# Second stage of a gated cross-attention kernel: down weights turned by transposing transfers, token factors in three bf16 parts, clip after rounding, first products by halves

## The chip, the cores and the metric

The kernel runs on one core of one Trainium2 chip. The metric is the device time of one execution in microseconds (us). Three runs of the kernel before gave 1939.12, 1939.28 and 1939.48 us; the median is 1939.28 us. The trace is of a further, profiled execution.

## The reference, cut to what matters

Two gated layers act on x of 4 x 1024 tokens with 512 features: a cross-attention over 64 text tokens with tanh, a quantized gated feed-forward, a second cross-attention with 16 heads, and a ternary feed-forward with a depthwise convolution. The part around the change is the quantized gated feed-forward:

```python
def _act_fake_quant(x, clip_factor):
    scale = sigmoid(clip_factor) * max(abs(x)) / 127.0
    return clip(round(x / scale), -128, 127) * scale
def _weight_fake_quant(w):
    scale = max(abs(w), axis=1) / 127.0
    return clip(round(w / scale), -128, 127) * scale
xq   = _act_fake_quant(x, clip_x[0])                       # x: layer-normed, 4096 x 512
gate = einsum('bsh,ih->bsi', xq, _weight_fake_quant(w_gate))   # 1408 x 512
up   = einsum('bsh,ih->bsi', xq, _weight_fake_quant(w_up))
h    = _act_fake_quant(silu(gate) * up, clip_down[0])
out  = einsum('bsi,hi->bsh', h, _weight_fake_quant(w_down))    # 512 x 1408
```

The scale of xq is one number for all tokens, and so is that of h: each needs the maximum over everything before the first value can be quantized. The weights w1 and w2 of the ternary feed-forward are also prepared here: mean of |w| over the whole matrix, then round(w / mean) clipped to -1, 0, 1.

## The kernel before, in words

The program has three stages on the same five engines; the order on each engine is written out by hand, one function for each engine and stage (`vector_A`, `vector_B`, `vector_C` and so on), and semaphores tie them. Stage A (up to about 963 us) is the first cross-attention; stage B (about 963 to 1151 us) computes silu(gate) * up and prepares weights; stage C is the rest. All DMAs are issued by SyncE (SP), in program order, each behind its own waits.

Between A and B stands a short chain. The layer norm's factor of every token, `ln1_scale` (128 tokens x 32 tiles), is turned by TensorE (L712) and copied to `cT` (L482); the largest value goes through `diagA` (L480) and a product with ones (L714) to all partitions, and VectorE forms `q_scale` (L484 to L490) and from it the scales `gs` and `us` (L867, L868).

Stage B works on four blocks of 1024 tokens, each in two halves of 512. The block index is o, and within a block i runs over 11 groups of 128 inner channels; n = 11 o + i runs from 0 to 43. For a half, TensorE spreads the token factors over the partitions (`rows`, four fp32 products of 128 columns, L1036), VectorE multiplies (`scaled`, L876), clips (L883) and rounds to bf16 (L888) into `xqT`. These three steps of block o + 1 stand behind the steps i = 2, 3, 4 and 6, 7, 8 of block o; for block 0 they stand ahead of the loop. For each n, TensorE forms 8 products for gate (L1060) and 8 for up (L1066), each 128 x 512; gate of n waits for h of n - 2, up of n waits for silu of n - 1. ScalarE computes silu (L1021), VectorE silu * up into `h` (L916) and the row maxima (L920), and SP stores h (L1156) to DRAM.

Beside this, three chains run in slots of n:

- Down weights, in four groups r of 128 rows, one group each 11 steps: load, VectorE's row maximum (L897), scale and reciprocal, ScalarE's scaling with the rounding constant (L987), eleven 128 x 128 fp32 transposes on TensorE in three turns through PSUM bank 7 (L1047), each copied by ScalarE to bf16 `wdT` (L991).
- Ternary weights, first pass from n = 1: 16 parts of 512 KB are loaded (L1125) into a ring of four buffers, ScalarE takes |w| (L1000), GpSimd adds it up (L1094); behind n = 19 VectorE sums over the columns (L933, twice), behind n = 20 TensorE spreads the sums through bank 6 (L1076), and behind n = 21 VectorE forms the means (L937, L940).
- Ternary weights, second pass: the same 16 parts are loaded again; from n = 23 ScalarE scales and rounds one part in each step (L1007), GpSimd clips it (L1098), and two steps later ScalarE writes fp8 (L1014). The load of a part waits for the fp8 write that frees its buffer; in SP's order it stands one step after that write and one step ahead of its use.

At the end the maximum of `hmax` goes through `diagB` (L955) and a product with ones (L1083) to `q_scale`, and stage C's first loads of h wait for `b_done`.

## Time and profile before

| | |
|---|---|
| median of three runs | 1939.28 us |
| profiled execution, its own time | 1936.77 us |
| span of its trace | 1934.9 us |
| mean granted TensorE clock in the span | 0.982 of full |
| TensorE busy | 1589.2 us, 82% |
| VectorE busy | 1715.7 us, 89% |
| ScalarE busy | 1477.4 us, 76% |
| GpSimd busy | 612.7 us, 32% |

The profiled execution lies 2.51 us below the median of the runs, and its span 1.87 us below its own time. PE is TensorE, PEld its weight loads, DVE VectorE, ACT ScalarE, POOL GpSimd, SPq SyncE's queue. A row of the timeline gives the start, the duration, the engine, the line, the operation, the tiles written and read, how many alike were merged, and in brackets the idle time just before with what ended it. A merged row of k instructions gives the time from the first start to the last end.

### The profile page before, as it was taken

To read this page: it belongs to the slowest core of one execution; us is meant where nothing else is said; L and a number is where in the kernel's file an instruction comes from. 1 tells how busy PE (TensorE), PEld (TensorE's weight loads), DVE (VectorE), ACT (ScalarE), POOL (GpSimd) and SP (SyncE) were. 2 spreads that over 40 slices of the span, in tenths; PEclk is the share of its full clock that TensorE was granted. 3 is DMA by queue.
4 is the path that set the end of the run, shared out by engine and by line. 5 is a ranking of instruction groups with operands and counts; after the bars stand their busy time and mean duration, and the time that the engine had idled before them with its cause. 6 is when DMAs were issued, how large, how long until landed. Compare 5 with 4: busy or idle time off the path is not lost.

```text
span 1934.9 us, 24513 instructions
## 1 busy us (share of the span) xinstructions
PE 1589.2 (82%) x9474; PEld 721.2 (37%) x9542; DVE 1715.7 (89%) x2616; ACT 1477.4 (76%) x1099; POOL 612.7 (32%) x480
## 2 busy tenths in 40 slices
PE   7778965698557976696499977999999987899996
PEld 4222211132112211231144434666666653444442
DVE  6999999999999998889688877899999867999997
ACT  4999999999999999999544754555454436888881
POOL 1000000000000000000043225666666643899991
PEclk9999999999999999999889989999999999999999
DMA  5001100020000010000079754333333111122212
GB/s 204 1 22 32 57 12 1 23 77 18 6 1 1 17 60 1 1 6 6 16 270 341 278 192 148 99 109 115 114 99 111 44 55 39 44 77 77 66 55 76
DMA packets 116709, 143.65 MB, mean 74 GB/s; under 512 B 25326, under 2 KB 74606, under 8 KB 116210
## 3 DMA queue, kind: packets, MB, share of 16 engines
q1 hardware_dynamic: 116594, 142.10, 22.3%
q8 instruction: 75, 1.23, 0.3%
q14 instruction: 40, 0.33, 0.1%
HBM read 87.55 MB, written 50.33 MB: 71 GB/s over the span
## 4 chain that ended last, share of the span: by engine, by line
ACT 44%; PE 32%; DVE 14%; POOL 4%; issue 4%; DMA 3%; SPq 0%; another core or an unknown queue 0%; DVEq 0%; POOLq 0%; ACTq 0%
ACT unit L546 40%; PE psum L1729 5%; PE psum L1763 5%; PE psum L1715 3%; PE psum L1066 3%; PE psum L1060 3%; DVE unit L457 2%; POOL h L1904 2%; PE psum L1739 2%; PE psum L1756 2%; DVE psum L1495 2%; PE psum L1786 1%; DVE psum L1500 1%; POOL hidden L1921 1%; PE psum L1748 1%
## 5 line engine op out<-in xcount | busy, mean ns | idle before, releaser
L546 ACT ACTIVATE unit<-unit 128x4096 f32<-128x4096 f32 x244 | 857.5, 3613 | 0.5 <-DVE unit L457 0.3
L457 DVE TENSOR_SCALAR unit<-feat_proj,text_proj 128x1024 f32<-128x1024 f32 x976 | 667.9, 749 | 64.3 <-PE psum L686 61.5
L686 PE MATMUL psum<-unit,w_pad 128*32 128x512 f32 x3904 | 471.8, 601 | 226.5 <-ACT unit L546 226.3
L686 PEld LDWEIGHTS psum<-unit,w_pad 128*32 128x32 f32 x3904 | 102.2, 109 | 542.0 <-ACT unit L546 384.9
L729 POOL TENSOR_SCALAR red<-red 128x8 f32<-128x8 f32 x4 | 2.0, 507 | 531.5 <-DVE red L332 531.5
L1786 PE MATMUL psum<-xq_block,w_q 128*128 128x512 bf16 x489 | 121.3, 388 | 16.1 <-ACT h L1662 11.2
L1904 POOL TENSOR_TENSOR h<-h,arow 128x512 f32<-128x512 f32 x104 | 125.5, 1231 | 20.4 <-ACT h L1662 20.4
L729 POOL TENSOR_SCALAR rstd<-mv 128x8 f32<-128x8 f32 (+1 forms) x5 | 1.7, 334 | 403.2 <-DVE mv L227 403.2
L598 PE MATMUL psum<-xnT,W_sb 128*128 128x512 f32 x256 | 123.4, 610 | 1.9 <-ACT xnT L500 1.9
L1637 ACT ACTIVATE scores<-scores 128x1024 f32<-128x1024 f32 x32 | 33.9, 1058 | 114.0 <-POOL scores L1890 114.0
L1921 POOL TENSOR_TENSOR hidden<-hidden,srow 128x2048 f32<-128x2048 f32 x28 | 114.3, 4083 | 10.1 <-DVE hidden_q L1530 9.8
L1729 PE MATMUL psum<-xnT_c,wq_sb 128*128 128x256 f32 x512 | 115.7, 379 | 1.2 <-ACT xnT_c L1624 1.2
L1763 PE MATMUL psum<-wo_sb,attn_outT 128*128 128x512 f32 x256 | 115.4, 593 | 0.0
L1818 PE MATMUL psum<-w_q,hidden_q 128*128 128x512 fp8e4 x448 | 101.3, 379 | 13.5 <-DVE x3in L1543 9.1
L1729 PEld LDWEIGHTS psum<-xnT_c,wq_sb 128*128 128x128 f32 x512 | 96.0, 190 | 20.2 <-issue 6.7
L1679 ACT ACTIVATE hidden<-psum 128x512 f32<-128x512 f32 x112 | 69.5, 640 | 27.3 <-DVE psum L1500 27.3
L1715 PE MATMUL psum<-wdT,hq 128*128 128x512 bf16 x323 | 78.7, 393 | 14.1 <-DVE hq L1427 11.1
L1667 ACT ACTIVATE psum<-h,conv_b_sb,conv_w_sb 128x512 f32<-128x512 f32 x112 | 86.6, 791 | 2.4
L1495 DVE SCALAR_TENSOR_TENSOR psum<-h,conv_w_sb,psum 128x512 f32<-128x512 f32 x112 | 82.9, 750 | 5.8 <-ACT psum L1667 5.7
L1060 PE MATMUL psum<-xqT,wgT 128*128 128x512 bf16 x348 | 84.0, 384 | 4.7 <-DVE xqT L888 3.7
L1021 ACT ACTIVATE silu<-psum,gs 128x1024 f32<-128x1024 f32 x44 | 48.7, 1108 | 49.8 <-PE psum L1060 47.3
L1066 PE MATMUL psum<-xqT,wuT 128*128 128x512 bf16 x340 | 83.3, 383 | 0.9 <-ACT silu L1021 0.3
(260 smaller groups left out, 2761.0 us busy)
## 6 DMA issues: line engine op xcount, KB each, us to landing
h_scratch<-h SPq DMA_DIRECT2D x44, 512.0 KB, 4.2
hin<-h_scratch SPq DMA_DIRECT2D x32, 704.0 KB, 4.7
xin<-in_x SPq DMA_DIRECT2D x8, 1024.0 KB, 5.7
tern_in<-in_w1T SPq DMA_DIRECT2D x16, 512.0 KB, 5.1
tern_in<-in_w2T SPq DMA_DIRECT2D x16, 512.0 KB, 7.0
x<-in_x SPq DMA_DIRECT2D x16, 512.0 KB, 3.7
x_scratch<-x SPq DMA_DIRECT2D x32, 256.0 KB, 2.0
x3in<-x_scratch SPq DMA_DIRECT2D x31, 256.0 KB, 3.0
```

The costliest lines, as they stand in the source:

```text
L457: ins = ve.tensor_scalar(units[:, n % 3, k, :], FP[:, bi % 2, k, :], TP[:, k, n:n + 1], None, ALU.add)
L546: ac.activation(units[:, n % 3], units[:, n % 3], ACT.Tanh).then_inc(unit_tanh, 1)
L598: mm = te.matmul(psum[:, banks[j], :], W_sb[:, k, m * P:(m + 1) * P], xnT[:, k, half * BANK:(half + 1) * BANK], start=(k == 0), stop=(k == ...
L686: mm = te.matmul(psum[k * TG:(k + 1) * TG, 3 + 2 * grp + half, :], w_pad[:, k, TG - 1 - tt:2 * TG - 1 - tt], units[:, n % 3, k, half * BAN ...
L1060: mm = te.matmul(gate_pair(n)[:, half, :], wgT[:, k, i * P:(i + 1) * P], xqT[:, o % 2, k, half * BLK:(half + 1) * BLK], start=(k == 0), st ...
L1066: mm = te.matmul(up_pair(n)[:, half, :], wuT[:, k, i * P:(i + 1) * P], xqT[:, o % 2, k, half * BLK:(half + 1) * BLK], start=(k == 0), stop ...
L1715: mm = te.matmul(psum[:, i, :], hq[:, i, c, :], wdT[:, c, :], start=(c == 0), stop=(c == NI - 1))
L1729: mm = te.matmul(psum[:, 2 + i, j * GRP:(j + 1) * GRP], wq_sb[:, k, m * P:(m + 1) * P], xnT_c[:, k, :], start=(k == 0), stop=(k == KC - 1))
L1763: mm = te.matmul(psum[:, 6, :], oT[:, i, k, :], wo_sb[:, k, :], start=(k == 0), stop=(k == KC - 1))
L1786: mm = te.matmul(raw_bank(n), w1_q[:, k, c * P:(c + 1) * P], xqb[:, f % 2, k, :], start=(k == 0), stop=(k == KC - 1))
L1904: gp.tensor_tensor(h1[:, c, 2:BANK + 2], h1[:, c, 2:BANK + 2], arow[:, f % 2, :], ALU.mult).then_inc(mid_gp, 1)
L1921: gp.tensor_tensor(H2[f % 2][:, :, cols, :], H2[f % 2][:, :, cols, :], srow[:, cols].unsqueeze(1).unsqueeze(3).broadcast_to([P, HC // 2, P ...
```

## The change

- The four spreads of a half use bf16: `ln1_scale` is turned by four fp32 products into four groups of 32 partitions, and VectorE splits it into a high, a middle and a low bf16 part in `cT` (128 x 128, bf16), with the second group masked by zeros in the selector `row_sel`. The spread is one bf16 product over 128 partitions for each tile. `diagA` and `diagB` go: the maximum itself, broadcast, is the stationary operand and the identity the moving one.
- `scaled` is made in two pieces of two feature chunks each, in two steps of i; `rounded` comes next and writes bf16, and `clipped` works on the bf16 values in place. The slots become i = 1, 2, 3, 4 and 5, 6, 7, 8; `rows` stand at i = 0 and 4.
- `gs` and `us` are formed by GpSimd.
- The products of n = 0 and gate of n = 1 are issued by halves: gate 0, up 0, gate 1 of the first half, then of the second.
- Down weights: ScalarE writes the rounded rows as bf16 `wd_bf`, SP stores them to DRAM, and eleven transposing DMAs (512 x 128 bf16 each) fill `wdT`, two in each of the steps n = 36 to 40 and one in n = 41. One group takes 9 steps. `diagD` moves from n = 37 to n = 31. TensorE's transposes and ScalarE's copies from PSUM go.
- The two column sums stand behind n = 13 and n = 19, the spread of the sums behind n = 21 (bank 7), the means behind n = 22, and the second ternary pass starts at n = 24.

The diff, cut to its core:

```diff
+        high, low = slice(2 * NT, P), slice(3 * NT, P)
         V.wait_ge(scale_mm, 1)
-        ve.tensor_copy(cT[:, :], psum[0:NT, 3, 0:P]).then_inc(scale_step, 1)
+        ve.tensor_copy(cT[:, :], psum[:, 3, 0:P]).then_inc(scale_step, 1)
+        V.wait_ge(scale_step, 2)
+        ve.tensor_tensor(rest[high, :], psum[high, 3, 0:P], cT[high, :], ALU.subtract).then_inc(scale_step, 1)
+        V.wait_ge(scale_step, 3)
+        ve.tensor_copy(cT[high, :], rest[high, :]).then_inc(scale_step, 1)
+        V.wait_ge(scale_step, 4)
+        ve.tensor_tensor(cT[low, :], rest[low, :], cT[low, :], ALU.subtract).then_inc(scale_step, 1)
...
-        te.transpose(psum[0:NT, 3, 0:P], ln1_scale[:, :], ident[:, :]).then_inc(scale_mm, 1)
-        T.wait_ge(scale_step, 2)
-        te.matmul(psum[:, 2, 0:P], ones[:, :], diagA[:, :], start=True, stop=True).then_inc(scale_mm, 1)
+        for c in range(P // NT):
+            mm = te.matmul(psum[c * NT:(c + 1) * NT, 3, 0:P], ln1_scale[:, :], ident[:, :], start=True, stop=True,
+                           tile_position=(0, c * NT))
+        mm.then_inc(scale_mm, 1)
+        T.wait_ge(scale_step, 1)
+        te.matmul(psum[:, 2, 0:P], red[:, 0, 0:1].broadcast_to([P, P]), ident[:, :], start=True,
+                  stop=True).then_inc(scale_mm, 1)
...
-    CLIP_SLOT, ROUND_SLOT = (3, 7), (4, 8)
-    SCALE_SLOT, ROW_SLOT = (2, 6), (1, 5)
-    DOWN_TURN = ((5, 0, 4), (7, 4, 8), (9, 8, NI))
+    SUMMED_SLOT = (13, MEAN_SLOT - 1)
+    ROUND_SLOT, CLIP_SLOT = (3, 7), (4, 8)
+    SCALE_SLOT, ROW_SLOT = (1, 5), (0, 4)
+    XQ_STEPS = 4
+    DOWN_EVERY = 9
...
+        def clipped(o, half):
+            xq = xqT[:, o % 2, :, half * BLK:(half + 1) * BLK]
+            V.wait_ge(xq_step, XQ_STEPS * (2 * o + half) + 3)
+            ve.tensor_scalar(xq, xq, QMAX, -QMAX - 1.0, ALU.min, ALU.max).then_inc(xq_step, 1)
...
+                if s == 5:
+                    A.wait_ge(wd_quant, r + 1)
+                    A.wait_ge(wd_moved, 16 * r)
+                    ac.activation(wd_bf[:, :], row, ACT.Copy, bias=-MAGIC).then_inc(wd_rounded, 1)
...
-                mm = te.matmul(psum[:, 6, f * P:(f + 1) * P], ident[0:NT, t:t + 1].broadcast_to([NT, P]), cT[:, :],
+                mm = te.matmul(psum[:, 6, f * P:(f + 1) * P], row_sel[:, t:t + 1].broadcast_to([P, P]), cT[:, :],
                                start=True, stop=True)
...
+            if n == 0:
+                for half in range(2):
+                    gate(0, half)
+                    up(0, half)
+                    gate(1, half)
...
+        def store_down(r):
+            S.wait_ge(wd_rounded, r + 1)
+            sp.dma_start(wd_dram[r * P:(r + 1) * P, :], wd_bf[:, :]).then_inc(wd_moved, 16)
+
+        def turn_down(c):
+            S.wait_ge(wd_moved, DOWN_STORED)
+            sp.dma_start(wdT[:, c, :], wd_dram[:, c * P:(c + 1) * P], transpose=True).then_inc(wd_moved, 16)
...
+            for r in range(KC):
+                if n == DOWN_EVERY * r + 7:
+                    store_down(r)
+            for c in range(NI):
+                if n == DOWN_EVERY * (KC - 1) + 9 + c // 2:
+                    turn_down(c)
```

## Rows read from the trace of the kernel before

**Rows 1.** Chain of waits, stages A to C: start, us, engine, tile, line.
```profile
987.37 1.73 PE psum L1060 x8
...
1056.52 2.27 DVE wsum L933 x2
...
1115.58 5.78 DMA tern_in<-in_w2T
...
1148.25 0.30 DVE diagB L955
```

**Rows 2.** Busy us by stretch: PE, PEld, DVE, ACT, POOL; clock; DMA share; GB/s.
```profile
970.00:979.00 9.00, 6.04 (x15) 1.98 (x15) 4.31 (x3) 2.40 (x2) 0.00 (x0) 0.52 0.70 239
979.00:1145.50 166.50, 161.39 (x772) 77.96 (x785) 145.65 (x127) 104.97 (x107) 58.01 (x32) 1.00 0.79 283
```

**Rows 3.** Groups by line in stage B: busy us, mean ns, idle before.
```profile
L916 DVE SCALAR_TENSOR_TENSOR h<-psum,us,silu 128x1024 f32<-128x1024 f32 x44 | 56.3, 1280 | 23.9 <-PE psum L1066 16.8 <-ACT silu L1021 5.8 <-issue 1.2
...
L883 DVE TENSOR_SCALAR xblk<-xblk 128x2048 f32<-128x2048 f32 x6 | 7.7, 1279 | 0.0
L1036 PE MATMUL psum<-ln_scaleT,ident 32*128 32x128 f32 x49 | 7.3, 285 | 0.0
L888 DVE TENSOR_SCALAR xqT<-xblk 128x2048 bf16<-128x2048 f32 x6 | 7.3, 1217 | 0.0
L1047 PE MATMUL psum<-ident,wd_row 128*128 128x128 f32 x44 | 6.9, 276 | 0.1
L897 DVE TENSOR_REDUCE down_scale<-wd_row 128x1 f32<-128x1408 f32 x4 | 6.4, 1609 | 0.0
```

**Rows 4.** Timeline, VectorE's h at n = 0, 22, 31, 32, 43.
```profile
979.38 1.28 DVE L916 SCALAR_TENSOR_TENSOR h<-psum,us,silu 128x1024 f32<-128x1024 f32 x1 [5.00 <-PE psum L1066]
...
1066.23 1.28 DVE L916 SCALAR_TENSOR_TENSOR h<-psum,us,silu 128x1024 f32<-128x1024 f32 x1 [0.65 <-PE psum L1066]
...
1104.06 1.28 DVE L916 SCALAR_TENSOR_TENSOR h<-psum,us,silu 128x1024 f32<-128x1024 f32 x1
1106.51 1.27 DVE L916 SCALAR_TENSOR_TENSOR h<-psum,us,silu 128x1024 f32<-128x1024 f32 x1
...
1145.45 1.28 DVE L916 SCALAR_TENSOR_TENSOR h<-psum,us,silu 128x1024 f32<-128x1024 f32 x1 [1.24 <-PE psum L1066]
```

**Rows 5.** Timeline, the passage from stage A to stage B.
```profile
961.76 0.27 DVE L482 COPY ln_scaleT<-psum 32x128 f32<-32x128 f32 x1
961.90 0.79 PE L714 MATMUL psum<-diagA,ones 128*128 128x128 f32 x2 [0.35 <-DVE diagA L480]
964.73 2.35 DVE L876 SCALAR_TENSOR_TENSOR xnT<-xnT,q_scale,psum 128x2048 f32<-128x2048 f32 x1 [0.86 <-PE psum L1036]
974.44 1.89 PE L1060 MATMUL psum<-xqT,wgT 128*128 128x512 bf16 x4 [2.83 <-DVE xqT L888]
976.41 1.28 ACT L1021 ACT_TABLE_LOAD   x1 [18.46 <-PE psum L1060]
```

**Rows 6.** Timeline of stage C: a bf16 clip, and GpSimd beside it.
```profile
1159.13 0.53 DVE L1427 TENSOR_SCALAR hq<-hq 128x1408 bf16<-128x1408 bf16 x1
...
1240.57 1.79 POOL L1880 TENSOR_TENSOR x<-x,down_out 128x512 f32<-128x512 f32 x1 [0.70 <-DVE down_out L1431]
...
1241.26 1.48 DVE L1427 TENSOR_SCALAR hq<-hq 128x1408 bf16<-128x1408 bf16 x1
```

**Rows 7.** GpSimd's additions of line 1094 alone: busy us, clock, DMA share, GB/s.
```profile
978.80:1045.90 67.10, 40.30 (x16) 1.00 0.83 301
```

**Rows 8.** Transposing DMAs of stage C: issue ns min/median/max, start, and landing.
```profile
L1961 SPq DMA_TRANSPOSE xq_block<-xq_scratch x32: 1122/1261/2005, 1576.9 to 1810.6; - x32
...
DMA to landing us min/median/max: 2.6/2.8/4.3
```

**Rows 9.** Timeline, ScalarE's scaling of the first and the sixteenth ternary part.
```profile
1068.91 1.14 ACT L1007 ACTIVATE tern_in<-tern_in,w_mean 128x1024 f32<-128x1024 f32 x1
...
1128.72 1.14 ACT L1007 ACTIVATE tern_in<-tern_in,w_mean 128x1024 f32<-128x1024 f32 x1
```

More of the change, by code:

```diff
@@ L141, in flamingo @@
     red = sb("red", [P, 12, TPB], stack=pa)
-    diagA = sb("diagA", [P, P], stack=pa)
+    rest = sb("ln1_scale_rest", [P, P], stack=pa)
     small_q = sb("small_q", [P, 2, 2 * NI], stack=pa)
@@ L218, in vector_A @@
         ve.tensor_reduce(sel[:, :], ident[:, :].rearrange("p (c j) -> p j c", j=TG), AX.X, ALU.add).then_inc(start_step, 1)
+        V.wait_ge(start_step, 2)
+        for part in (slice(0, NT), slice(2 * NT, P)):
+            ve.tensor_copy(row_sel[part, :], sel[part, :])
         def moments(bi, i):
@@ L866, in vector_B, with scaled @@
     def vector_B():
-        ve.tensor_scalar(gs[:, :], gate_scale[:, :], q_scale[:, 0:1], None, ALU.mult)
-        ve.tensor_scalar(us[:, :], up_scale[:, :], q_scale[:, 0:1], None, ALU.mult).then_inc(a_done, 1)
-        def scaled(o, half):
+        def scaled(o, half, part):
             q = 2 * o + half
@@ L907, in vector_B @@
         for half in range(2):
-            scaled(0, half)
+            scaled(0, half, 0)
+            scaled(0, half, 1)
+            rounded(0, half)
             clipped(0, half)
-            rounded(0, half)
         for n in range(NH):
@@ L1053, in tensor_B, with product, gate, up @@
         T.wait_ge(kv_copied, KC + NB)
+        def product(bank, w, n, half):
+            o, i = divmod(n, NI)
+            T.wait_ge(xq_step, XQ_STEPS * (2 * o + half + 1))
+            for k in range(KC):
+                mm = te.matmul(bank[:, half, :], w[:, k, i * P:(i + 1) * P],
+                               xqT[:, o % 2, k, half * BLK:(half + 1) * BLK], start=(k == 0), stop=(k == KC - 1))
+            return mm
+        def gate(n, half):
+            T.wait_ge(h_done, 2 * (n - 2) + 1)
+            mm = product(gate_pair(n), wgT, n, half)
+            if half == 1:
+                mm.then_inc(gate_mm, 1)
+        def up(n, half):
+            T.wait_ge(silu_done, n)
+            mm = product(up_pair(n), wuT, n, half)
+            if half == 1:
+                mm.then_inc(up_mm, 1)
         for n in range(NH):
             o, i = divmod(n, NI)
-            T.wait_ge(h_done, 2 * (n - 2) + 1)
-            for half in range(2):
-                T.wait_ge(xq_step, 3 * (2 * o + half + 1))
-                for k in range(KC):
-                    mm = te.matmul(gate_pair(n)[:, half, :], wgT[:, k, i * P:(i + 1) * P],
-                                   xqT[:, o % 2, k, half * BLK:(half + 1) * BLK], start=(k == 0), stop=(k == KC - 1))
-            mm.then_inc(gate_mm, 1)
-            T.wait_ge(silu_done, n)
-            for half in range(2):
-                for k in range(KC):
-                    mm = te.matmul(up_pair(n)[:, half, :], wuT[:, k, i * P:(i + 1) * P],
-                                   xqT[:, o % 2, k, half * BLK:(half + 1) * BLK], start=(k == 0), stop=(k == KC - 1))
-            mm.then_inc(up_mm, 1)
+            if n == 0:
[3 more added lines that the diff above has]
+                    gate(1, half)
+            else:
+                for half in range(2):
+                    if n > 1:
+                        gate(n, half)
+                for half in range(2):
+                    up(n, half)
             for half in range(2):
@@ L1080, in tensor_B @@
         mm.then_inc(down_row_mm, 1)
-        T.wait_ge(hscale_step, 2)
-        T.wait_ge(wd_copied, 3 * KC)
-        te.matmul(psum[:, 7, 0:P], ones[:, :], diagB[:, :], start=True, stop=True).then_inc(hscale_mm, 1)
+        T.wait_ge(hscale_step, 1)
+        T.wait_ge(mean_done, 1)
+        te.matmul(psum[:, 7, 0:P], wred[:, 4:5].broadcast_to([P, P]), ident[:, :], start=True,
+                  stop=True).then_inc(hscale_mm, 1)
     def gpsimd_B():
-        G.wait_ge(a_done, 1)
+        G.wait_ge(scale_step, 8)
+        gp.tensor_scalar(gs[:, :], gate_scale[:, :], q_scale[:, 0:1], None, ALU.mult)
+        gp.tensor_scalar(us[:, :], up_scale[:, :], q_scale[:, 0:1], None, ALU.mult).then_inc(a_done, 1)
         G.wait_ge(kv_mm, KC + NB)
```

105 lines of the change are left out of this document (41 added, 64 removed).

## The prediction

> **What bounds the kernel now.** I read the chain of waits first, then busy time by stretch, then the groups of lines of stage B, then single instructions. Nothing outside 961 to 1151 us is touched, so only stage B and the passage into it count. In the chain, stage B is TensorE for most of its length, in trains of 8 products that take 1.73 us [rows 1]; one n costs 2 x 1.73 = 3.46 us. By stretch, TensorE is busy 161 of 166.5 us after 979 us, but VectorE 146 as well, and the DMA engines carry 283 GB/s at a share of 0.79 [rows 2]: three resources stand close together. From h of n = 0 (979.38) to h of n = 22 (1066.23) pass 86.85 us [rows 4], of which 22 x 3.46 = 76.1 are products. The other 10.7 are the four spreads and six turns in that stretch (records of 285 and 276 ns before overlap, [rows 3]) and a stop while VectorE sums twice, 2.27 us [rows 1]. From n = 22 to 43 pass 79.22 us [rows 4] for 21 x 3.46 = 72.7 us of products; there the chain shows ScalarE's ternary parts and waits for their loads, such as 5.78 us at 1115.58 [rows 1]. So the first half is bound by TensorE, the second by a ring of loads with TensorE close behind.
>
> **The change, part by part.**
>
> *Passage into stage B.* `scaled` starts at 964.73 [rows 5]. The new turn is four fp32 products side by side; nothing shows these. I take the 0.79 us of L714, between the nothing that a hidden turn costs and four of them in a row, 3.2. From the start of the old turn, 0.6 us ahead of the copy L482, that gives 961.95. Four dependent VectorE steps, each like L482 (0.27 and some 0.03 between), end at 963.1; the three steps of `q_scale` take about 0.8 as now. The product that replaces `diagA` and L714 runs meanwhile, and so do the bf16 spreads. `scaled` starts at about 964.0, 0.7 early. The first half then costs two pieces like L916 (1.28 each: half of the elements, one operand in PSUM), a round of 1.22 [rows 3] and a clip. Clip on bf16: 0.53 us for 1408 elements with GpSimd quiet [rows 6], which for 2048 is at most 0.77; I take 0.70. It can't cost less than 0.53, and 1.22 (L888) if no faster path is taken. Sum 4.5 and small gaps: the first half is ready at 968.55 and the second at 973.0, against 974.44 now [rows 5]. In between TensorE forms 12 products that it now forms later. At 970 to 979 the granted clock is 0.52 [rows 2], the 1.2 GHz level, after little work; at 979 it is full. With 12 products at the low clock, twice 0.216 us each, TensorE is at 973.7 and ends gate of n = 0 near 974.5. Silu follows with its table load (1.28, [rows 5]) and about 1.1 us: h of n = 0 starts near 977.0 instead of 979.38: **-2.4 us** (-1 to -3.5, by the clock and the turn). GpSimd's `gs` and `us` are needed only by then.
>
> *n = 0 to 21.* TensorE now needs 22 x 3.46 = 76.1 us and four spreads of at most 1.1 each. The turns are gone, and the spread of the sums waits for nothing, since it stands two steps behind the second sum. VectorE takes its place. Its list for 22 steps: h and row maximum 22 x 2.45 = 53.9 (1104.06 to 1106.51 where nothing else stands between, [rows 4]); four halves of 2 x 1.28 + 1.22 + 0.70 = 4.48, 17.9; three row maxima of down weights (n = 1, 10, 19) of 1.61 with 0.3 for scale and reciprocal, 5.7; two sums, 2.3 [rows 1, 3]. Together 79.9 against 86.85: **-6.95 us**. If clips cost 1.22, four of them and the two at the entry give 3.1 back.
>
> *A wait that the list leaves out.* In stage C the same clip takes 1.48 instead of 0.53 us when GpSimd is 0.69 us into an addition of 1.79 [rows 6]: it gave up 0.95 of the 1.10 us that the addition still had to go. Rounds and clips at n = 3, 4, 7, 8, 14 and 15 meet GpSimd's additions of the first pass: 16 of them, 2.52 us each, 40.3 of 67.1 us [rows 7]. Today those twelve steps of L883 and L888 average 1.28 and 1.22 us with 1.22 the usual size [rows 3]: they happen to start while GpSimd is idle or ahead of it. All slots move, and VectorE now trails. A start at random waits 16 x 2.52 x 2.52 / 2 / 67.1 = 0.76 us on average, six of them 4.5 us; the bounds are 0 (as today) and 6 x 2.52 = 15. I take the average, since neither the old phase nor the worst one is kept: **+4.5 us**. Behind a waiting clip stand h of the next n on VectorE, and behind that TensorE's gate two steps on; VectorE is the bound here, so nothing hides it.
>
> The Trainium skill, SBUF — State Buffer, "Who interferes with whom", says that a VectorE instruction in a two-port mode and a GpSimd instruction exclude each other and that the second to start waits for the whole of the first. The trace agrees within 0.15 us (0.95 of 1.10). With that rule left out the stage would come out 4.5 us earlier, which is the first rival.
>
> *n = 22 to 43.* The second ternary pass starts at n = 24, one step later. In a stretch led by VectorE, silu of 24 comes after gate of 24, which waits for h of 22: 1.28 + 1.73 + 0.2, and silu before the first scaling, 1.0: it starts 4.2 us after h of 22; now 1068.91 - 1066.23 = 2.68. From the first scaling to the sixteenth pass 59.8 us [rows 9]; the ring of four buffers, a load at each turn and the same VectorE beside it stay, so I keep 59.8. From the sixteenth to h of 43 are 16.73 us now, one step of 3.46 less afterwards: 13.3. Sum 77.3 against 79.22, -1.9. ScalarE's two extra passes over a group (1408 elements each) replace three copies from PSUM, and `diagD` falls where VectorE already waits for loads: nothing for both, covered by those waits.
>
> *Turns by transfer.* Four stores of 0.36 MB and eleven transfers of 0.13 MB. A transposing transfer takes SP 1.26 us to issue (1.12 to 2.0) and lands after 2.8 us (up to 4.3) [rows 8]. SP has 2 x 1.26 in a step of 3.5 us beside one store of h and, until n = 38, one load. Its own waits for h cover that: the last turn is issued in n = 41, behind h of 40, and lands some 7 us later, while h of 43 and the maximum take over 10. What stays are ternary loads behind two transposes in the DMA engines in n = 37 and 38. I add 0.5 us (0 to 2). Together **-1.4 us**. At the end `diagB` goes, 0.30 and a gap [rows 1]: **-0.35**.
>
> **Sum:** -2.4 - 6.95 + 4.5 - 1.4 - 0.35 = -6.6 us against the profiled execution's 1936.77, so 1930.2; the median of runs lies 2.51 higher: **1932.7 us**.
>
> **Rivals.** (a) *No collisions.* Rounds and clips again find GpSimd idle, for instance because the additions shift by the same amount as VectorE. For it: today's twelve steps; against it: the slots move against the additions. The 4.5 go: -11.1, 1928.2 us.
>
> (b) *The ring eats the gain.* The same bytes in a shorter stage, 2.9 MB of down weights on top, at a share of 0.79 already [rows 2]: a load that lands 1 us later costs half a microsecond in each part that waits for it, since two steps lie between the write that frees a buffer and the use. If the landing grows from the 4 to 5.8 us now seen in the chain by 1.7 us on some 8 parts, 6.8 us go: 0 net, 1939.3 us. Against it: 0.79 leaves a fifth free, and the chain has only few DMA pieces today.
>
> (c) *SP can't issue the turns in time: slower.* The place is n = 36 to 41 on SP. From h of 35 to the point where VectorE would wait for the last turn lie some 33 us, of which 2.8 go to six stores and two loads and 4.3 to the last landing: 26 for eleven turns, 2.35 us each. Below that nothing shows; above it each 0.1 us costs 1.1. At 3.5 us each (other transfers in the same queue hold them up) it is +12.7, net +6: 1945.4 us, and the first loads of stage C stand behind them. Against it: 2.0 us is the most seen in 32 cases, though at a lower DMA load [rows 8].
>
> That the clip is no faster on bf16 is inside the range of the forecast (3.1 us).
>
> **How the numbers follow.** Forecast 0.46, (a) 0.22, (b) 0.20, (c) 0.12. The range runs from 1927 (rival (a) with the best entry) to 1941 (rival (b) and its margin); it leaves out most of (c). The forecast's own range is 1929 to 1936.5. 0.2% is 3.9 us, about what a measurement of this kernel can tell from no change. Faster: 0.85 of the forecast and all of (a), with a little of (b): 0.63. Slower: (c) and a little of the rest, 0.14. Same: 0.23.
>
> **What would show it.** h of n = 0 near 977; VectorE without gaps from there to n = 22 and h of 22 near 1061.5 (1057 for (a)); rounds and clips of 1.5 to 3 us beside GpSimd's additions (L883 and L888 have 1.22 today); TensorE with waits for h instead of for sums; the bf16 spreads well under 1.1 us for a half; h of 43 near 1139; the last turn landed before the last maximum. Wrong it would be if the entry gains nothing because the low clock lasts, if clips keep 1.22 us, or if ScalarE's waits for ternary loads grow beyond a microsecond each.

## The result, and the profile after

The changed kernel takes 1924.27 us (median of 1923.63, 1923.91, 1924.63 and 1925.59) where before took 1939.28: a ratio of 0.9932 (0.992 to 0.9944), 15 us. The forecast was 1932.7, with 1927 as the low end of its range: the direction was right, and the gain about twice the 6.6 forecast. In the later comparisons, on other chips, before had medians of 1936.6 to 1938.1 and single executions from 1934.2 to 1940.5, so the gain is some 12 to 15 us: `e1_again`, beside before on one chip, gave 1924.29 against 1936.61. All times here are of undisturbed executions; two of one experiment (2419 and 3250 us) were not, and are left out.

The table cuts the profiled execution at the first maximum of stage A's scales (L483, `red<-ln_max`), at h of n = 0, 22 and 43, and at the first load of stage C. Each entry is a difference of two starts.

| us | own time | start to maximum | to h of 0 | to h of 22 | to h of 43 | to stage C | stage C |
|---|---|---|---|---|---|---|---|
| before | 1936.77 | 961.34 | 18.04 | 86.85 | 79.22 | 5.87 | 783.58 |
| after | 1925.59 | 964.26 | 15.30 | 79.15 | 78.84 | 5.38 | 780.57 |
| difference | -11.18 | +2.92 | -2.74 | -7.70 | -0.38 | -0.49 | -3.01 |

The edits lie in the four columns from the maximum to stage C: -11.3. The outer two differ by 1.9 and 1.8 between two executions of the changed kernel (`e1_again`), and by as much as here among its variants.

The timeline of after: the maximum, the spread and the first scaling of the passage, and h of n = 0, 22 and 43 (start, us, engine, line).

```profile
964.26 0.18 DVE L483 TENSOR_REDUCE red<-ln_max 128x1 f32<-128x32 f32 x1
...
966.06 0.61 PE L1047 MATMUL psum<-ln_scaleT,row_sel 128*128 128x128 bf16 x4 [0.60 <-DVE ln_scaleT L493]
...
966.81 1.28 DVE L891 SCALAR_TENSOR_TENSOR xnT<-xnT,q_scale,psum 128x1024 f32<-128x1024 f32 x1
...
979.56 1.28 DVE L933 SCALAR_TENSOR_TENSOR h<-psum,us,silu 128x1024 f32<-128x1024 f32 x1 [3.92 <-ACT silu L1034]
...
1058.71 1.28 DVE L933 SCALAR_TENSOR_TENSOR h<-psum,us,silu 128x1024 f32<-128x1024 f32 x1
...
1137.55 1.28 DVE L933 SCALAR_TENSOR_TENSOR h<-psum,us,silu 128x1024 f32<-128x1024 f32 x1 [0.91 <-PE psum L1058]
```

The spread of a half takes 0.61 us in the passage, the first half is scaled 2.55 us after the maximum (before 3.39, [rows 5]).

Busy us by stretch, after (columns as in [rows 2]).

```profile
970.00:979.00 9.00, 7.19 (x27) 3.03 (x28) 5.54 (x6) 1.87 (x2) 0.00 (x0) 0.69 0.88 315
979.00:1138.00 159.00, 150.53 (x695) 67.47 (x710) 143.13 (x133) 105.30 (x100) 57.49 (x32) 1.00 0.92 319
```

In the passage the granted clock is 0.69 on average against 0.52: part of it now runs at the upper level, with 27 TensorE instructions instead of 15. In stage B TensorE is busy 95% of the stretch, VectorE 90%, and the DMA engines carry 319 GB/s at a share of 0.92 against 283 at 0.79.

Groups of stage B, after, against [rows 3].

```profile
L933 DVE SCALAR_TENSOR_TENSOR h<-psum,us,silu 128x1024 f32<-128x1024 f32 x44 | 56.2, 1278 | 17.7 <-ACT silu L1034 15.3 <-PE psum L1058 2.3
...
L898 DVE TENSOR_SCALAR xqT<-xblk 128x2048 bf16<-128x2048 f32 x6 | 8.7, 1444 | 0.0
...
L904 DVE TENSOR_SCALAR xqT<-xqT 128x2048 bf16<-128x2048 bf16 x6 | 4.1, 683 | 0.0
...
L1047 PE MATMUL psum<-ln_scaleT,row_sel 128*128 128x128 bf16 x20 | 1.9, 219 | 0.0
```

The clip takes 683 ns instead of 1279. The spread's products fell from 285 to 219 ns each, and no longer share TensorE with 44 turns. VectorE's h waits 15.3 us for silu where it waited 16.8 for TensorE. And the round takes 1444 ns on average where it took 1217: that is two rounds, one of 2.08 us at n = 14 and one of 1.71 in the second half, and all that is to be seen of the collisions.

The stretch from h of n = 0 to h of n = 22 by itself (columns as above).

```profile
979.56:1058.71 79.15, 76.27 (x356) 34.22 (x364) 77.81 (x71) 44.73 (x42) 40.80 (x16) 1.00 0.94 353
```

VectorE is busy 77.81 of 79.15 us; in between, its timeline has one wait for another engine, 0.45 us for silu at n = 5. TensorE, with 76.27, is close behind.

The timeline of the changed kernel at the places where rounds and clips (L898, L904) and GpSimd's additions (L1113) come near each other: n = 4, 7 and 14.

```profile
996.96 0.68 DVE L904 TENSOR_SCALAR xqT<-xqT 128x2048 bf16<-128x2048 bf16 x1
...
997.13 2.73 POOL L1113 TENSOR_TENSOR w_acc<-w_acc,tern_in 128x1024 f32<-128x1024 f32 x1 [5.93 <-ACT tern_in L1013]
...
1005.38 2.37 POOL L1113 TENSOR_TENSOR w_acc<-w_acc,tern_in 128x1024 f32<-128x1024 f32 x1
...
1007.82 1.22 DVE L898 TENSOR_SCALAR xqT<-xblk 128x2048 bf16<-128x2048 f32 x1
...
1030.68 2.37 POOL L1113 TENSOR_TENSOR w_acc<-w_acc,tern_in 128x1024 f32<-128x1024 f32 x1 [0.83 <-ACT tern_in L1013]
...
1032.05 2.08 DVE L898 TENSOR_SCALAR xqT<-xblk 128x2048 bf16<-128x2048 f32 x1
```

At n = 4 the clip starts 0.17 us ahead of the addition: the clip takes its 0.68 us, the addition 2.73 instead of 2.37. At n = 7 the addition ends at 1007.75 and the round starts at 1007.82. In the first half only the round at n = 14 came while an addition was under way, for 1.37 us then, and it took 0.86 us more. This one collision is what the forecast had at six times 0.76.

### The profile page after: what moved, and what is told of

It reads as the page before. It is cut to its first block, busy times and chain, and to the rows that moved or that the text cites. A ratio compares the mean times of both kernels' runs of the same rounds, so it can differ in the third digit from the quotient of the medians.

```text
span 1923.5 us, 24394 instructions
## 1 busy us (share of the span) xinstructions
PE 1577.8 (82%) x9406; PEld 708.5 (37%) x9473; DVE 1713.1 (89%) x2626; ACT 1476.9 (77%) x1091; POOL 613.9 (32%) x482
## 3 DMA queue, kind: packets, MB, share of 16 engines
q8 instruction: 75, 1.23, 0.3%
## 4 chain that ended last, share of the span: by engine, by line
ACT 44%; PE 30%; DVE 14%; issue 4%; POOL 4%; DMA 3%; SPq 1%; DVEq 0%; ACTq 0%; POOLq 0%
ACT unit L557 41%; PE psum L1762 5%; PE psum L1796 5%; PE psum L1058 4%; PE psum L1748 3%; DVE unit L463 2%; POOL h L1937 2%; PE psum L1772 2%; PE psum L1789 2%; PE psum L1819 2%; DVE psum L1528 1%; DVE psum L1533 1%; POOL hidden L1954 1%; PE psum L1781 1%; PE psum L609 1%
## 5 line engine op out<-in xcount | busy, mean ns | idle before, releaser
L1528 DVE SCALAR_TENSOR_TENSOR psum<-h,conv_w_sb,psum 128x512 f32<-128x512 f32 x112 | 82.7, 748 | 5.4 <-ACT psum L1700 5.3
L1533 DVE SCALAR_TENSOR_TENSOR psum<-h,conv_w_sb,psum 128x512 f32<-128x512 f32 x112 | 82.1, 747 | 0.0
```

## The experiments

After each: its median, and the two halves of stage B (h of n = 0 to 22, and 22 to 43) in its profile. The medians come from four chips, on which before's own medians lie up to 1.5 us apart; the halves, which differ by 0.2 between the two profiles of the changed kernel, are read first.

**e1_again**: the changed kernel unaltered. 

> The changed kernel, nothing altered: the base of the experiments, and a second look at two differences that lie outside the edited stage. In the profiled pair, stage A became 2.96 us longer (its first eight projection products take 5.80 instead of 3.69 us) and stage C 3.0 us shorter (780.6 instead of 783.6). If these differ from execution to execution, the first comes out anywhere between 3.7 and 5.8 us and stage C anywhere from 780.6 to 783.6, and the time against before is 0.993. If the change causes them (another order of code and of the buffers), stage A shows 5.8 us again and stage C 780.6 again. Stage B by every theory: h of n = 0 to n = 22 in 79.2 us, n = 22 to 43 in 78.8.

1924.29 us, ratio 0.9936 (0.9924 to 0.9949); 79.35 and 78.63. The maximum stands at 962.39, stage C takes 782.3. Over the fifteen profiles of the changed kernel and its variants, the maximum stands at 961.4 to 964.5 and stage C takes 780.5 to 784.8. Two executions of this one kernel differ by 1.9 and 1.8 there. So +2.92 and -3.01 in the table lie within what is seen without any edit to these stages, and they cancelled by chance.

**e9_before**: before unaltered, for a second profile. 

> The kernel before, unaltered, for a second profile of it. In six profiles of the changed kernel and its variants, stage C took 780.5 to 782.8 us and stage A ended (first row of maxima of ln1) between 961.5 and 964.3; before showed 783.6 and 961.3 once. If stage C got shorter by the change, it shows 783.5 again, more than 0.7 above all of those; if it differs only from execution to execution, it falls among them. Stage B has to show 86.9 and 79.2 us again, within 0.4.

1936.38 us; 86.85 and 79.56; maximum at 961.36; stage C 782.86, among those of the changed kernel. So stage C is not seen to get shorter by the change.

**e2_short_adds**: GpSimd's additions cut to 64 columns. 

> GpSimd's sixteen additions of the first ternary pass shortened from 1024 to 64 elements a partition (fifteen sixteenths of the sum are left out, so the means and what is made of them differ). It removes what rounds and clips can wait for. The forecast's term (six collisions of 0.76 us on average, 4.5 us) expects h of n = 0 to n = 22 to shrink from 79.15 by about 4.5 us, to 74.7. The rival (the additions have fallen in step with VectorE and hold it up only where L898 shows 2.08 and 1.71 instead of 1.22 us, 1.35 in all) expects 77.8, no less than 77.5. Either way n = 22 to 43 stays at 78.8 within 0.5, if anything a little longer, since its ring of loads starts earlier.

```diff
-gp.tensor_tensor(acc, acc, tern_in[:, part % 4, :], ALU.add)
+gp.tensor_tensor(acc[:, 0:64], acc[:, 0:64], tern_in[:, part % 4, 0:64], ALU.add)
```

GpSimd's group in the first half (columns as in [rows 3]).

```profile
L1113 POOL TENSOR_TENSOR w_acc<-w_acc,tern_in 128x64 f32<-128x64 f32 x16 | 6.0, 374 | 60.6 <-ACT tern_in L1013 60.6
```

6.0 us of additions instead of some 40, and the first half takes 78.38 (second 78.58; 1923.42 us, ratio 0.9936, 0.9922 to 0.9949). All additions together cost 0.8 to 1.0 us. The forecast's 4.5 falls; the rival's bound (no less than 77.5) holds.

**e3_late_adds**: each addition waits for h of its step. 

> One added wait: GpSimd starts the addition of part p only when VectorE has ended h of the same step (n = p + 1), so that each addition (2.36 us) begins with the row maximum (1.22 us) and lies across the round or clip behind it. Nothing is left out. If a round or clip does wait for an addition that began before it, and only its place in the step has spared it, each of the six rounds and clips at n = 3, 4, 7, 8, 14 and 15 now waits about 2.36 - 1.22 = 1.14 us: 6.8 us more minus the 1.35 that it already has, h of n = 0 to 22 about 84.6 and the kernel +5.5 us. If the additions cost VectorE little wherever they lie, it stays at 79.2 within 1 us. If they had been at random places already, as the forecast took it (4.5 us), it becomes 81.5.

```diff
 G.wait_ge(part_abs, part + 1)
+G.wait_ge(h_done, 2 * (part + SUM_SLOT) + 1)
```

Its timeline at n = 3, and h of n = 22.

```profile
989.23 2.35 POOL L1114 TENSOR_TENSOR w_acc<-w_acc,tern_in 128x1024 f32<-128x1024 f32 x1 [1.33 <-DVE h L933]
...
990.27 2.40 DVE L898 TENSOR_SCALAR xqT<-xblk 128x2048 bf16<-128x2048 f32 x1
...
1062.19 1.28 DVE L933 SCALAR_TENSOR_TENSOR h<-psum,us,silu 128x1024 f32<-128x1024 f32 x1 [1.63 <-issue]
```

The 16 products of n = 22 ahead of that h, as busy us by stretch (columns as in [rows 2]): the changed kernel, then this one.

```profile
1054.99:1058.62 3.63, 3.63 (x19) 1.74 (x20) 3.60 (x5) 1.11 (x1) 0.00 (x0) 1.00 1.05 409
```

```profile
1056.78:1062.09 5.31, 5.31 (x19) 2.17 (x20) 3.74 (x5) 2.34 (x2) 0.00 (x0) 0.68 1.06 389
```

85.68 and 78.90; 1931.56 us, 7.3 above `e1_again`. The addition is under way by 1.04 us when the round comes and has 1.31 to go; the round takes 1.18 more. Five of the six rounds and clips show that 1.18 (2.40 or 1.86 us); at n = 4 the part comes late anyway (its addition starts 0.18 us behind the clip). 5 x 1.18 = 5.9 in place of 0.9 to 1.05, 4.9 of the 6.4 that the first half lost. The rest is TensorE's clock: the granted clock falls from 1.00 to 0.50 (the 1.2 GHz level) behind the last sum, the 16 products take 5.31 us instead of 3.63, and h of n = 22 waits 1.63. TensorE had stood 0.88 and 0.81 us around the product of the sums, exactly as in the changed kernel, whose clock stays at 1.00; no run shows why it fell here. The wait of the forecast exists at full price: what failed is how often it falls due.

**e10_adds_after_max**: the same wait one instruction later. 

> The changed kernel with the wait of the run of late additions moved by one instruction: GpSimd adds part p when VectorE has ended the row maximum of step p + 1, not h. A round or clip that follows the maximum then always starts ahead of the addition, and the addition is the one that waits. If who starts first decides who pays, no round or clip exceeds 1.25 and 0.75 us in n = 0 to 17, L898's 2.08 at n = 14 goes, and h of n = 0 to 22 takes 78.4 (as with the short additions); against 85.7 for a wait that ends 1.22 us earlier. If both engines lose when they meet, it stays above 80.

```diff
+G.wait_ge(h_done, 2 * (part + SUM_SLOT) + 2)
```

Its timeline at n = 14.

```profile
1029.96 1.22 DVE L898 TENSOR_SCALAR xqT<-xblk 128x2048 bf16<-128x2048 f32 x1
...
1030.18 3.23 POOL L1114 TENSOR_TENSOR w_acc<-w_acc,tern_in 128x1024 f32<-128x1024 f32 x1 [2.39 <-DVE hmax L937]
```

78.29 and 78.69 (1924.09 us; ratio 0.9929, 0.9914 to 0.9944). The addition starts 0.22 us behind the round and is the one that is stretched (3.23 us); all rounds and clips of the first half take 1.22 and 0.68. With `e3_late_adds` this is one instruction's difference in a wait and 7.4 us in the stage, 5.9 of them collisions and most of the rest the clock there. The Trainium skill, SBUF — State Buffer, "Who interferes with whom", says it in a sentence: "Issue order, not op shape, decides who blocks." Both runs agree.

**e7_clip_f32**: clip on fp32 values ahead of the round again. 

> The changed kernel with the clip before the round on fp32 values again (1.22 us as L883 before, instead of 0.68 on bf16). Two clips lie on the way into the stage (+1.1 us to h of n = 0) and four between n = 0 and 22. Theory 1 (VectorE's list is the bound of the first half, as the forecast had it: each clip costs in full): +2.2 us there, 81.4, the kernel +3.3. Theory 2 (TensorE and VectorE are about equal and a clip hides in VectorE's waits for silu, 4.4 us in the first half): 79.2 to 80, the kernel +1.1 to 1.9.

```diff
-rounded(0, half); clipped(0, half)      # clip on xqT, bf16
+clipped(0, half); rounded(0, half)      # clip on the fp32 block
```

The 16 products of n = 22 (as for `e3_late_adds`).

```profile
1056.48:1061.69 5.21, 5.21 (x19) 2.11 (x20) 3.74 (x5) 1.69 (x2) 0.00 (x0) 0.69 1.05 404
```

82.23 and 78.67; passage 16.06 against 15.0 to 15.8 in the variants that leave it alone; 1927.84 us, 3.6 above `e1_again` (forecast 3.3). VectorE's busy time in the first half grows by 2.14 us, four clips at 0.54, and its timeline is without a gap up to h of n = 22: VectorE's list does bind there. That the half grew by 2.9 to 3.1, and that the kernel came so near the forecast, is in part the clock: it falls to 0.50 here too, the 16 products take 5.21 us instead of 3.63, and h of n = 22 waits 1.52 for silu. Without that wait the half is 1.4 to 1.6 longer, since the 0.45 at n = 5 is used up first. One clip of 2.21 us beside an addition takes the place of the round of 2.08.

**e6_f32_spreads**: token factors spread from an fp32 row again. 

> The changed kernel with the token factors spread from the fp32 row again (32 contracted partitions, fp32 products) instead of the three bf16 parts; one copy more (0.27 us) in front of the passage. A half's four products then take up to 1.1 us on TensorE instead of 0.39. Theory 1 (TensorE is the bound of the first half or within a microsecond of it): 4 x 0.7 = 2.8 us more there, h of n = 0 to 22 about 81.0 to 82; the entry 0.3 to 1.4 later; the second half the same; the kernel +2 to +4. Theory 2 (VectorE hides them): 79.2 to 79.7, and the kernel +0.3 to +1.5.

```diff
-te.matmul(..., row_sel[:, t:t + 1].broadcast_to([P, P]), cT[:, :], ...)
+te.matmul(..., ident[0:NT, t:t + 1].broadcast_to([NT, P]), cT32[:, :], ...)
```

Its first spread in the passage.

```profile
964.06 2.07 PE L1049 MATMUL psum<-ln_scaleT,ident 32*128 32x128 f32 x8 [0.78 <-DVE ln_scaleT L495]
```

A half's spread is 2.07 us in the passage, 0.61 in the changed kernel. 80.23 and 80.50, passage 16.89; 1930.67 us. The halves lose 1.0 and 1.8, the passage 1.5: theory 1's total by the trace (4.3), but 1.8 of it in the second half, where it expected none; there the second ternary pass starts 7.33 us behind h of n = 22 instead of 6.36. The profiled execution was one of its two lowest, 1.4 below the median; the remaining 2 us of the median are not located.

**e11_sums_together**: both sums at n = 19 as before. 

> The changed kernel with both row sums of the ternary accumulators at n = 19 and the mean on TensorE at n = 20, as before, instead of sums at n = 13 and 19 and the mean at 21. TensorE has to wait for both sums behind the row maximum of n = 19, where before its stop took 2.27 us. If the first half is bound by TensorE and VectorE together, the stop costs 1.2 to 2.3 us: h of n = 0 to 22 80.4 to 81.4 and the kernel +1 to +2. If VectorE alone bounds it, the stop is made up for before n = 22, and it stays at 79.2 within 0.4.

```diff
-SUMMED_SLOT = (13, MEAN_SLOT - 1)       # mean at n = 21
+SUMMED_SLOT = (MEAN_SLOT - 1, MEAN_SLOT - 1)   # mean at n = 20
```

Its chain of waits at n = 19.

```profile
1046.35 1.53 DVE down_scale L912
...
1047.88 2.27 DVE wsum L951 x2
```

The products behind the sums (columns as in [rows 2]), and before's at the same place.

```profile
1050.65:1059.19 8.54, 8.54 (x35) 3.61 (x34) 4.75 (x8) 2.81 (x3) 0.00 (x0) 0.80 0.69 261
```

```profile
1058.83 0.38 PE L1076 MATMUL psum<-wsum,ones 128*128 128x2 f32 x2 [3.24 <-DVE wsum L933]
```

82.54 and 78.61, the first half 3.2 to 3.4 longer. TensorE stands behind the last row maximum of down weights and both sums, 3.8 us in one place (4.11 us of idle time). Then its granted clock falls to 0.50 for some 3 us: the next 31 products take 8.54 us, which at the full clock (3.46 for 16) take 6.7. So about 1.8 of the loss is the clock, and the stop itself 1.4 to 1.6, within the first theory's 1.2 to 2.3. Before stood 3.24 us at its sums and kept a clock of 1.00 [rows 2], so the stop alone does not explain the fall. The median, 1931.21, is 6.9 above `e1_again`; its profiled execution (1927.56) was its fastest.

**e5_turns_back**: down weights turned by TensorE and copied by ScalarE as before. 

> The changed kernel with the down weights as before: transposes on TensorE by three groups to a row block (n = 11 r + 5, 7, 9), copies by ScalarE, no stores or turns by transfer; the mean of the ternary sums keeps its new place in bank 7, and waits for the sixth copy. All else as changed. In the changed kernel TensorE has 22 x 3.46 + 4 x 0.39 = 77.7 us of products and spreads in the 79.2 us between h of n = 0 and 22. Theory 1 (TensorE bound the first half, and the turns were most of what it lost): 22 transposes of at most 0.28 us come back into that stretch, 4 to 6 us, so 83 to 85; n = 22 to 43 within 1 us of 78.8, since the ring of ternary loads bounds it; the kernel +4 to +6. Theory 2 (VectorE bounds the first half, and the gain came from the spreads and the separated sums): 79.2 to 80.7, the kernel +1.5 at most.

```diff
-store_down, turn_down on SP; wd_bf on ScalarE
+te.transpose(psum[:, 7, ...], wd_row[...], ident) ; copies from PSUM on ScalarE
+T.wait_ge(wd_copied, 6)                 # ahead of the mean in bank 7
```

The first half (columns as in [rows 2]), the turns' group in it, and ScalarE's waits for ternary loads from 1056 to 1138 us (us in total, times, longest): first this kernel, then the changed one, then the one with five buffers, below.

```profile
978.53:1058.89 80.36, 78.29 (x377) 37.04 (x386) 75.61 (x68) 44.70 (x46) 39.31 (x16) 1.00 0.91 333
```

```profile
L1062 PE MATMUL psum<-ident,wd_row 128*128 128x128 f32 x22 | 3.5, 278 | 0.7 <-ACT wd_row L1002 0.7
```

```profile
ACT tern_in L1022 <- DMA tern_in<-in_w1T: 1.6, 3, 1.0
...
ACT tern_in L1022 <- DMA tern_in<-in_w2T: 1.3, 3, 0.7
```

```profile
ACT tern_in L1020 <- DMA tern_in<-in_w2T: 5.1, 4, 1.8
...
ACT tern_in L1020 <- DMA tern_in<-in_w1T: 1.5, 3, 0.7
```

80.36 and 76.84; 1924.91 us, the same as the changed kernel. 22 turns are 3.5 us of TensorE, and the first half takes 1.0 to 1.2 more. That is theory 2's range, but not its reason: this run also takes work from VectorE, since with row blocks every 11 steps two row maxima of down weights instead of three fall into the half, and no round meets an addition. VectorE is busy 75.61 us instead of 77.81, TensorE 78.29 instead of 76.27, and h now waits for TensorE. So with the turns TensorE binds the half, and what the turns cost beside an unchanged VectorE was not run. The second half is 1.8 to 2.0 shorter. Turning by transfers, the part with the largest diff, brings nothing net: what it frees on TensorE it costs in waits for loads, 6.6 us in total against 2.9.

**e4_ring5**: five ternary buffers (and five of h). 

> The ring of ternary parts with five buffers instead of four (paid for by five instead of six buffers of h), so that each load of the second pass is issued one step of some 3.6 us earlier. If the second half is bound by that ring, as the forecast has it, ScalarE's waits for ternary loads in the chain (5.76 us at 1119.72 and others) shrink, and h of n = 22 to 43 falls from 78.8 towards the 72.7 us that its 42 trains of products need, by 2 to 5 us; the kernel gains as much. If something else sets the second half (VectorE, or TensorE with the spreads), it stays within 0.7 us of 78.8. If five buffers of h are too few, VectorE waits for stores of h and it becomes longer, which the waits would name.

```diff
-tern_in = sb("tern_in", [P, 4, PART]);  HR = 6
+tern_in = sb("tern_in", [P, 5, PART]);  HR = 5
```

ScalarE's waits, same stretch: these two rows are all there are.

```profile
ACT silu L1035 <- PE psum L1059: 12.6, 14, 2.3
...
ACT wd_row L1003 <- DVE down_inv L921: 3.2, 2, 2.5
```

79.15 and 75.97; 1920.53 us, 3.8 below `e1_again`, ratio 0.9916 (0.9902 to 0.9929). The waits for ternary loads are gone, 2.7 to 2.9 us of the second half with them. The ring bound it, as forecast.

**e12_turns_back_ring5**: both. 

> Down weights turned on TensorE as before, and five ternary buffers with five of h. With four buffers the turns on TensorE took 80.36 us for the first half (against 79.2) and 76.84 for the second (against 78.8 with transfers). If the transfers cost the second half time only by way of the ring of ternary loads, the fifth buffer helps little here: 75.5 to 76.5, near the 75.97 of five buffers with transfers. If they cost by something else as well (ScalarE's two passes over a group, traffic on the DMA engines), it falls to 74 to 75.

80.37 and 78.09; 1928.68 and 1930.30 us. Neither theory: the second half got longer than with four buffers. Its chain shows why for most of it.

```profile
1088.56 1.18 DVE bo_row L963
...
1092.10 1.89 DVE xqT L899
```

The scaling of the bias row takes 1.18 us where `e5_turns_back` has 0.39, and the round 1.89 instead of 1.22: 1.46 us of waits on VectorE, as beside the additions, here at n = 28 and 29, where GpSimd clips ternary parts. That pair was not separated by a run of its own. No wait for a ternary load is left in this kernel either; why that brings nothing beside the 1.46 us is not located.

**e8_ring5_one_turn**: five buffers, and one turn to a step while ternary loads are issued. 

> The kernel with five ternary buffers, with the four row blocks of down weights taken every 8 steps instead of 9 and the first six turns issued one to a step (n = 33 to 38), so that SP never issues two turns between two ternary loads. If the turns in SP's queue delay the last ternary loads also with five buffers, h of n = 22 to 43 falls from 75.97 by 0.7 to 2 us. If the fifth buffer has already covered that (2.5 us of issue against one step of 3.6), it stays within 0.5 us, and the kernel at 1920.5 within 0.7.

```diff
-DOWN_EVERY = 9 ... if n == DOWN_EVERY * (KC - 1) + 9 + c // 2:
+DOWN_EVERY = 8 ... if n == DOWN_EVERY * (KC - 1) + 9 + (c if c < 6 else 6 + (c - 6) // 2):
```

80.52 and 75.74; 1924.99 us. The second half is that of `e4_ring5` within 0.25: with five buffers the turns are covered. The first is 1.4 longer, since a round at n = 14 now waits 2.07 us: the moved row block shifted the steps against the additions. The other 3 us of the median lie outside stage B in its profile: the maximum stands 2.4 later than in `e4_ring5`, and stage C takes 1.9 more.

**e14_one_turn**: the same with four buffers. 

> The changed kernel (four ternary buffers) with row blocks of down weights every 8 steps instead of 9, and the first six turns one to a step (n = 33 to 38), the other five from n = 39. In the changed kernel's chain SP issues four turns of 1.23, 1.25, 1.81 and 1.26 us between ternary loads at 1111.9 to 1119, and the last such load is then issued at 1119.7. If that queue on SP costs the second half, the load goes out some 2.5 us earlier and h of n = 22 to 43 falls from 78.6 - 78.8 by 1 to 2.5 us. If it is the landing of the loads (5.6 us in the chain at 1104.2, ahead of all turns) that binds them, it stays within 0.5. The first half may differ by up to 1.5 through the moved row blocks, as it did with five buffers (80.5).

 

The chain of the changed kernel from 1112 us, the first turn of each of two pairs, then the issue of the last ternary load and ScalarE's waits in this run.

```profile
1112.26 1.23 SPq L1143
...
1115.93 1.81 SPq L1143
...
1119.72 5.76 DMA tern_in<-in_w2T
```

```profile
1117.47 0.33 SPq L1152 DMA_DIRECT2D tern_in<-in_w2T  x1
```

```profile
ACT tern_in L1020 <- DMA tern_in<-in_w2T: 3.8, 6, 1.2
...
ACT tern_in L1020 <- DMA tern_in<-in_w1T: 0.5, 1, 0.5
```

79.41 and 76.19, 2.4 to 2.7 shorter; 1923.25 us. In the changed kernel SP issues pairs of turns (1.23 to 1.81 us each) between two ternary loads, and the last load goes out 61.0 us after h of n = 22; here 58.9 (1117.47 - 1058.60). Loads still end waits, 4.3 us in all, but the queue on SP was the larger part of the loss. The row blocks moved as well; with five buffers both edits together changed the second half by 0.23 (`e8_ring5_one_turn`).

**e15_plain_turn**: plain transfers of the same size in place of the transposing ones. 

> The changed kernel with its eleven transposing transfers replaced by plain ones of the same size, in the same places of the queue (the down weights then lie untransposed and in part repeated, so what is made of them differs). If the transposing transfers' time on SP (1.2 to 1.8 us each) or in the DMA engines costs the second half, it falls from 78.6 - 78.8 by 1 to 2.5 us, towards the 76.84 of turns on TensorE. If only the added bytes or ScalarE's two passes over a group count, it stays within 0.5.

```diff
-sp.dma_start(wdT[:, c, :], wd_dram[:, c * P:(c + 1) * P], transpose=True)
+sp.dma_start(wdT[:, c, :], wd_dram[c % KC * P:(c % KC + 1) * P, 0:D])
```

DMA view from 1100 to 1140 us, the changed kernel and this one (packets and bytes; queue, packets, MB, share of 16 engines).

```profile
DMA packets 8615, 10.88 MB, mean 272 GB/s; under 512 B 6275, under 2 KB 6275, under 8 KB 8613
...
q1 hardware_dynamic: 8613, 10.86, 91.6%
```

```profile
DMA packets 4178, 10.74 MB, mean 269 GB/s; under 512 B 464, under 2 KB 1872, under 8 KB 4176
...
q1 hardware_dynamic: 4176, 10.72, 75.5%
```

79.33 and 77.69; 1925.13 us. Between the theories: 0.9 to 1.2 us shorter, and the last ternary load goes out 59.9 us after h of n = 22 (1116.88 - 1056.94), between the 61.0 and 58.9 above. About the same bytes in transposing form are 6275 packets under 512 B instead of 464 and hold the engines for 91.6% of the stretch instead of 75.5%, and SP for 1.2 to 1.8 us each instead of 0.4 to 1.4 (median 0.45).

**e13_ring5_max_mask**: what the runs point to, in one kernel. 

> What the runs point to, together: five ternary buffers (five of h), additions that start behind the row maximum, and the two VectorE instructions on the mask and the bias row (0.34 and 0.39 us, n = 28, ahead of a round) moved to n = 35. From five buffers alone (79.15 and 75.97): the first half 78.3, the second 75.2 to 75.8; the kernel 1919 to 1920 where stage A and stage C fall as in that run (961.5 and 781.0), up to 3 us more where they fall late.

Its chain in the second half.

```profile
1086.09 1.67 DVE xqT L899
...
1106.44 10.74 PE psum L1059 x49
```

78.30 and 75.69, as expected; 1920.00 us, ratio 0.9908 (0.9891 to 0.9924), the lowest median of all, though `e4_ring5` alone, with 1920.53, can't be told from it. From 1099.7 us on, the chain is products without a gap (49 in 10.74 us). What it still shows is a round of 1.67 beside GpSimd's ternary clips.

## Why the prediction was wrong

**The sum.** 8.4 us too high in the median, in two parts. 3.8 came from the offset: I added 2.51, the distance of before's profiled execution from its median, but the profiled execution of after was 1.3 above its own. Start and stage C differ by 1.9 and 1.8 us between two profiles of one kernel, and by 3 and 4 over all variants, so one profile against three runs can't fix an offset of 2.5. The other 4.6 lie in stage B (own time 1925.59 against 1930.2 forecast), where four columns of the table give -11.3 against -6.6.

**The step that failed** is "a wait that the list leaves out": +4.5 us for six rounds and clips at random against GpSimd's additions, with the mean taken between 0 and 15. Measured: one collision, 0.86 in the profile, 0.8 to 1.0 for all additions (`e2_short_adds`, `e10_adds_after_max`). The price of a collision was right (1.18 at 1.31 still to go). The chance was not: an addition starts when ScalarE's absolute value ends, or behind another addition, and the steps of both engines repeat, so the phase is set by the order of work and not drawn. The variants bear that out: none in `e5_turns_back`, `e11_sums_together` and `e12_turns_back_ring5`, 0.84 to 1.05 in seven profiles (the changed kernel's too), 2.2 in `e8_ring5_one_turn`, 5.9 where I put the additions across the rounds. So rival (a), given 0.22, was the mechanism but for one collision; its 1928.2 was still 3.9 high by the offset. That its own time without the offset (1925.7) meets the measured 1925.59 is luck: VectorE's list was 1.6 too long, and the one collision and a second half 1.0 too short made up for it.

**VectorE's list** came out at 79.9; without collisions it is 78.3 to 78.4 (`e10_adds_after_max`, `e2_short_adds`). It summed busy times, and in the timeline instructions that stand behind each other overlap a little: from h of n = 8 to h of n = 9 with a clip between pass 3.05 us (1008.95 to 1012.00), where 2.45 and 0.70 make 3.15. Twenty-odd seams of some 0.08 (an estimate from this one) make the 1.6. That VectorE binds was right: it is busy 77.81 of 79.15 us, and the slower clips lengthened its list in full (`e7_clip_f32`). But TensorE stands so close behind that 2 us more of its work, with 2 us less of VectorE's, make it the bound (`e5_turns_back`).

**The passage**: -2.74 against -2.4; -2.3 to -3.0 in the variants that leave it alone. Steps as named; the spread is far below the 1.1 us for a half even at the low clock.

**The second half**: -0.38 against -1.4. The changed kernel's gate of n = 24, and ScalarE's scaling of the first and the sixteenth ternary part (before's in [rows 9]).

```profile
1062.13 1.89 PE L1058 MATMUL psum<-xqT,wgT 128*128 128x512 bf16 x8
```

```profile
1065.07 1.14 ACT L1020 ACTIVATE tern_in<-tern_in,w_mean 128x1024 f32<-128x1024 f32 x1
...
1125.50 1.15 ACT L1020 ACTIVATE tern_in<-tern_in,w_mean 128x1024 f32<-128x1024 f32 x1 [1.76 <-DMA tern_in<-in_w2T]
```

The term that was too small is the start: the first scaling comes 6.36 us after h of n = 22, not 4.2. I let gate of 24 follow h of 22 at once; but TensorE still has gate and up of 23 to do then, and gate of 24 starts 3.42 us after h of 22. From the first scaling to the sixteenth pass 60.43 us, with 60.3 in the forecast (59.8 and 0.5 for the transfers), and from there to h of 43 12.05 instead of 13.3. That the middle term came out is luck. I had SP's own waits for h cover the issue of the transfers, and they don't: two turns of 1.2 to 1.8 us between two ternary loads put the last load 2 us later, and with one turn to a step the first to the sixteenth part take 57.78 us (`e14_one_turn`). So the queue cost some 2.5 us, and the ring without it was 2.0 faster than the 59.8 that I kept; why, no run shows. Rival (b) had the loads late by a longer landing. The landing did not grow (median of the last twelve loads 4.3 us before, 4.4 after, at a share of 0.89 in that half against 0.71); the loads were issued later. Rival (c)'s limit of 2.35 us for a turn was not reached; the queue that it named was the right one, but who stood behind it were the ternary loads, not the last turn.

**The end**: -0.49 against -0.35.

**Which edits earned it**: undone one by one, the first half loses 3.3 (sums apart), 3.0 (clip), 1.1 (turns) and 1.0 (spreads). This is no split of the 7.7 gained: 1.8 of the first and 1.5 of the second are a clock of 0.50 that neither before nor the changed kernel had in this half, and the turns' figure is 2.0 us more of TensorE with 2.2 less of VectorE. What is left is some 1.5, 1.5, 1.1 and 1.0, 5.1 together, and how the rest of the 7.7 falls on the edits together was not run. The turns give theirs back in the second half.

## What to carry to other kernels

Where two engines block each other, don't average over phases: find in the timeline what starts each of the two instructions in that step, and see who comes second. If the patient one can be made to wait for the start of the other, a wait of one instruction settles it. When a run loses more than its edit accounts for, read the granted clock of each stretch before you look for another wait: in three runs here it was the missing 1.5 to 1.8 us. And when work moves from an engine to transfers, count what the queue that issues them holds back: the price stood on SP and in a ring of buffers, not on the engine relieved.

## What the runs showed of the hardware

A transposing transfer of 128 KB took SP 1.2 to 1.8 us to issue under load (a plain one 0.4 to 1.4), and landed after 4.2 us (median), as a plain one did (3.9); but it held the DMA engines longer, a share of 0.92 against 0.76 with about the same bytes. The Trainium skill, Advanced Engine Details and Errata, "X-Bar Transpose (TRN2)", says that transposing transfers are as fast as regular ones: so it is for the landing, not for the queue and the engines. Two profiles of the changed kernel differed by 1.9 us in a stage A that nobody touched and 1.8 us in stage C, and fifteen of it and its variants by 3 and 4 us. TensorE's granted clock fell to 0.50 behind the sums in three of these fifteen (`e3_late_adds`, `e7_clip_f32`, `e11_sums_together`), after TensorE had stood for 1.7 to 4.1 us; the changed kernel stood for 1.7 us and before for 3.24 at the same place and kept 1.00.
